# One full-width product for queries times key states, and a different order of the softmax weights' transfers and of GpSimd's splits

## The reference

```python
z = cumlogsumexp(s, axis=tokens);  g = exp(z_shifted - z);  p = exp(s - z)
# per head and token t, with the state hk (64 x 64):
hk = hk * g_t + k_t[:, None] * p_t[None, :];   ok_t = q_t @ hk          # scores against slots
pv = softmax(ok)                                                         # over the 64 slots
hv = hv * g_t[:, None] + p_t[:, None] * v_t[None, :];   ov_t = pv_t @ hv
o = ov * rsqrt(mean(ov**2) + eps) * g_norm * silu(x @ Wg);   out = o @ Wo
```

## Time and profile before

| | |
|---|---|
| time, median of 3 runs | 1357.21 us (1354.89 to 1357.36) |
| the profiled execution | 1352.27 us, its span 1350.5 us |
| PE busy | 1323.4 us (98%) |
| DVE busy | 1055.9 us (78%) |
| ACT busy | 425.9 us (32%) |
| POOL busy | 138.2 us (10%) |
| TensorE clock granted | 0.999 of full speed |

### The profile page before, as it was taken

How to read it: one execution, slowest core, us unless ns; L and a number is a source line. 1 busy time by engine, 2 the same in 40 slices (tenths; PEclk the granted TensorE clock), 3 DMA queues, 4 the chain that set the end, 5 groups by cost and what they waited for, 6 DMA issues and landing times.

```text
span 1350.5 us, 24275 instructions
## 1 busy us (share of the span) xinstructions
PE 1323.4 (98%) x9287; PEld 1096.4 (81%) x9287; DVE 1055.9 (78%) x1675; ACT 425.9 (32%) x1283; POOL 138.2 (10%) x106
## 2 busy tenths in 40 slices
PE   6999999999999999999999999999999999999998
PEld 5788888888888888888888888878888778888886
DVE  8888888888888888888988898888778764535354
ACT  4333323332332233233323333333223423222221
POOL 3012101110120011001101110111100000000000
PEclk9999999999999999999999999999999999999999
DMA  6147555655665565556655655575332620000000
GB/s 187 40 107 176 115 119 131 161 117 110 147 135 126 119 164 127 128 123 156 138 122 122 161 121 116 119 169 117 75 93 44 192 80 0 32 1 31 0 32 32
DMA packets 500559, 144.58 MB, mean 107 GB/s; under 512 B 359648, under 2 KB 491616, under 8 KB 500448
## 3 DMA queue, kind: packets, MB, share of 16 engines
q1 hardware_dynamic: 500448, 143.08, 45.4%
HBM read 85.80 MB, written 57.21 MB: 106 GB/s over the span
## 4 chain that ended last, share of the span: by engine, by line
PE 76%; DVE 10%; SPq 5%; DMA 5%; issue 3%; ACT 0%; POOL 0%; DVEq 0%
PE bank L486 15%; PE bank L488 14%; PE bank L487 14%; PE bank L118 13%; PE bank L1654 6%; PE bank L726 3%; SPq L369 3%; PE bank L709 2%; PE bank L566 2%; PE bank L546 2%; SPq L334 2%; DMA fp_weights<-q 1%; DMA e_tokens<-k_tok_then_wT 1%; PE bank L645 1%; PE bank L714 1%
## 5 line engine op out<-in xcount | busy, mean ns | idle before, releaser
L486 PE MATMUL bank<-wvg_hi,xT_hi 128*128 128x512 f32 x512 | 206.7, 404 | 0.7
L488 PE MATMUL bank<-wvg_hi,xT_lo 128*128 128x512 f32 x512 | 199.9, 390 | 0.0
L487 PE MATMUL bank<-wvg_lo,xT_hi 128*128 128x512 f32 x512 | 199.7, 390 | 0.0
L786 ACT ACTIVATE a_and_v<-bank 128x256 f32<-128x256 f32 x128 | 49.0, 383 | 332.9 <-PE bank L488 332.8
L486 PEld LDWEIGHTS bank<-wvg_hi,xT_hi 128*128 128x128 f32 x512 | 96.2, 188 | 25.5 <-issue 4.2
L488 PEld LDWEIGHTS bank<-wvg_hi,xT_lo 128*128 128x128 f32 x512 | 96.1, 188 | 20.6
L487 PEld LDWEIGHTS bank<-wvg_lo,xT_hi 128*128 128x128 f32 x512 | 96.3, 188 | 17.8
L1103 DVE RECIPROCAL cT<-cT 128x512 f32<-128x512 f32 x32 | 107.0, 3343 | 0.0
L1048 POOL TENSOR_TENSOR rstd<-ssq,neg_half 128x8 f32<-128x8 f32 x32 | 52.4, 1636 | 494.3 <-DVE ssq L1151 494.3
L486 PE MATMUL bank<-wo_hi,oT_hi 128*128 128x512 f32 x256 | 99.8, 390 | 0.0
L488 PE MATMUL bank<-wo_hi,oT_lo 128*128 128x512 f32 x256 | 99.6, 389 | 0.0
(11 more groups left out here) (164 smaller groups left out, 3029.1 us busy)
## 6 DMA issues: line engine op xcount, KB each, us to landing
o_transposed<-o SPq DMA_DIRECT2D x27, 512.0 KB, 3.4
oT_lo<-o_transposed SPq DMA_DIRECT2D x108, 128.0 KB, 3.0
fp_weights<-q SPq DMA_DIRECT2D x28, 318.0 KB, 3.4
e_tokens<-k_tok_then_wT SPq DMA_DIRECT2D x31, 256.0 KB, 2.3
e_tok<-e_tokens SPq DMA_DIRECT2D x124, 64.0 KB, 2.3
c_tokens<-cT SPq DMA_DIRECT2D x31, 256.0 KB, 2.4
cT<-c_tokens SPq DMA_DIRECT2D x124, 64.0 KB, 2.3
w_slots<-p SPq DMA_DIRECT2D x27, 256.0 KB, 2.4
```

The costliest lines, as they stand in the source:

```text
L486: pe.matmul(dst, w_hi, m_hi, start=(k == 0), stop=False)
L487: pe.matmul(dst, w_hi, m_lo, start=False, stop=False)
L488: last = pe.matmul(dst, w_lo, m_hi, start=False, stop=(k == n - 1))
L786: return act.activation(dst, src, ACT.Copy)
```

## The change

Three things are changed. (1) `hk` becomes 128 wide and is set to zero once: the state of head 0 goes to rows 0 to 63, columns 0 to 63, that of head 1 to rows 64 to 127, columns 64 to 127. One copy of ACT becomes two of 64 partitions. L673's 12 products of 64 x 64 by 64 columns per unit become 3 of 128 x 128 by 128 columns. ok of both heads now lies in T0 and is scaled by one DVE instruction instead of two; the parts of hv lie in T1, and their waits move. (2) In SP's queue `load_w` stands right behind `store_w`, and the k weights of the next pair and the loads of e behind it. (3) In units with i = 3 GpSimd's two low parts wait for `s_wm`, the end of L1296.

```diff
-    hk = sb("hk", [P, CH - 1, P])[:, :, 0:M]
+    hk = sb("hk", [P, CH - 1, P])
-    ok_of = [[t[:, c * M:(c + 1) * M] for c in range(CH)] for t in (T0, T1)]
+    ok_of = [T0[:, c * P:(c + 1) * P] for c in range(CH)]
+    hv_of = [T1[:, c * P:(c + 1) * P] for c in range(CH - 1)]
...
             load_q8(u)
-            if i == 2:
-                load_skq(pair, 1)
             store_e(u + 1)
             if u in W_FAR:
                 store_w(u)
+                load_w(u)
+            if i == 2:
+                load_skq(pair, 1)
             load_e(u + 1)
-            if u in W_FAR:
-                load_w(u)
...
             if c:
-                pe.wait_ge(s_hk, 3 * u + c)
+                pe.wait_ge(s_hk, 2 * (3 * u + c))
...
-                if beside is not None and out_bank(u, c) is state_banks(beside)[1]:
-                    pe.wait_ge(s_hv, (CH - 1) * (beside + 1))
...
-            pe.wait_ge(s_hk, 3 * (u + 1))
+            pe.wait_ge(s_hk, 2 * 3 * (u + 1))
             for c in range(1, CH):
-                for a in range(2):
-                    hs = slice(DK * a, DK * (a + 1))
-                    for h in range(2):
-                        ts, ds = slice(64 * h, 64 * (h + 1)), slice(c * P + 64 * h, c * P + 64 * (h + 1))
-                        mm = pe.matmul(ok_of[a][c][ts, :], qT[hs, ds], hk[hs, c - 1, :],
-                                       start=False, stop=True, skip_group_check=True)
+                mm = pe.matmul(ok_of[c], qT[:, c * P:(c + 1) * P], hk[:, c - 1, :],
+                               start=False, stop=True, skip_group_check=True)
...
-                out_product(v, range(CH), u)
+                out_product(v, range(CH))
+            pe.wait_ge(s_hv, 3 * (u + 1))
...
-            copy(hk[:, c, :], state_banks(u)[0][:, 0:M]).then_inc(s_hk, 1)
+            if not u and c == 0:
+                act.wait_ge(s_zero, 1)
+            for a in range(2):
+                rows = slice(64 * a, 64 * (a + 1))
+                copy(hk[rows, c, M * a:M * (a + 1)], hk_bank(u)[rows, 0:M]).then_inc(s_hk, 1)
...
                 pool.wait_ge(s_job, job_count(VG3, u, i))
+                pool.wait_ge(s_wm, u + 1)
                 for k in range(2, KT):
                     lo_vg(pair_of_next(u), k)
...
-            for a in range(2):
-                head = [t.rearrange("p (c a m) -> p c a m", a=2, m=M)[:, :, a, :] for t in (p[:, :], c_tok)]
-                dve.scalar_tensor_tensor(out=head[0], in0=(T0, T1)[a][:, 0:CH * M].rearrange("p (c m) -> p c m", m=M),
-                                         scalar=SCALE, in1=head[1], op0=ALU.mult, op1=ALU.mult).then_inc(s_oks, 1)
+            dve.scalar_tensor_tensor(out=p[:, :], in0=T0[:, :], scalar=SCALE, in1=c_tok,
+                                     op0=ALU.mult, op1=ALU.mult).then_inc(s_oks, 1)
...
+        dve.memset(hk[:, :, :], 0.0).then_inc(s_zero, 1)
```

More of the change, by code:

```diff
@@ L551, in key_sums @@
             if c:
-                pe.wait_ge(s_hk, 3 * u + c)
+                pe.wait_ge(s_hk, 2 * (3 * u + c))
             for a in range(2):
                 hs, at = slice(64 * a, 64 * (a + 1)), slice(M * a, M * (a + 1))
-                mm = pe.matmul(state_banks(u)[0][hs, 0:M], k_tok[:, c, at], e_tok[:, c, at], start=(c == 0), stop=True,
+                mm = pe.matmul(hk_bank(u)[hs, 0:M], k_tok[:, c, at], e_tok[:, c, at], start=(c == 0), stop=True,
                                skip_group_check=True)
             mm.then_inc(s_hkd, 1)
-        def inner_ok(par, chunks):
-            for c in chunks:
-                for a in range(2):
-                    at = slice(M * a, M * (a + 1))
-                    for h in range(2):
-                        ts = slice(64 * h, 64 * (h + 1))
-                        pe.matmul(ok_of[a][c][ts, :], av[par][:, a, c, 0, ts], e_tok[:, c, at],
-                                  start=(c == 0), stop=(c == 0), skip_group_check=True)
         def out_transposes(u, banks):
@@ L582, in w_transposes, with out_product @@
             mm.then_inc(s_trw, 1)
-        def out_product(u, chunks, beside=None):
+        def out_product(u, chunks):
             for c in chunks:
-                if beside is not None and out_bank(u, c) is state_banks(beside)[1]:
-                    pe.wait_ge(s_hv, (CH - 1) * (beside + 1))
                 cols = slice(c * P, (c + 1) * P)
@@ L639, in unit @@
             pe.wait_ge(s_v, (u + 1) * CH)
-            inner_ok(par, range(CH))
+            for c in range(CH):
+                for a in range(2):
+                    at = slice(M * a, M * (a + 1))
+                    for h in range(2):
+                        ts = slice(64 * h, 64 * (h + 1))
+                        pe.matmul(ok_of[c][ts, at], av[par][:, a, c, 0, ts], e_tok[:, c, at],
+                                  start=(c == 0 and a == 0), stop=(c == 0), skip_group_check=True)
             key_sums(u, 1)
@@ L644, in unit @@
                     hs, at = slice(64 * a, 64 * (a + 1)), slice(M * a, M * (a + 1))
-                    mm = pe.matmul(state_banks(u)[1][hs, c * DV:(c + 1) * DV], e_tok[:, c, at], av[par][:, a, c, 1, :],
+                    mm = pe.matmul(hv_of[c][hs, :], e_tok[:, c, at], av[par][:, a, c, 1, :],
                                    start=(c == 0), stop=(c == 0), skip_group_check=True)
@@ L662, in unit @@
                 pe.wait_ge(s_cinv, 1)
-                pe.wait_ge(s_hk, CH - 1)
                 for c in range(CH):
-                    mm = pe.transpose(A[0][:, c * P:(c + 1) * P], c_sum[:, c * P:(c + 1) * P], ident[:, :])
+                    mm = pe.transpose(A[1][:, c * P:(c + 1) * P], c_sum[:, c * P:(c + 1) * P], ident[:, :])
                 mm.then_inc(s_trc, 1)
-            pe.wait_ge(s_hk, 3 * (u + 1))
+            pe.wait_ge(s_hk, 2 * 3 * (u + 1))
             for c in range(1, CH):
-                for a in range(2):
-                    hs = slice(DK * a, DK * (a + 1))
-                    for h in range(2):
-                        ts, ds = slice(64 * h, 64 * (h + 1)), slice(c * P + 64 * h, c * P + 64 * (h + 1))
-                        mm = pe.matmul(ok_of[a][c][ts, :], qT[hs, ds], hk[hs, c - 1, :],
-                                       start=False, stop=True, skip_group_check=True)
+                mm = pe.matmul(ok_of[c], qT[:, c * P:(c + 1) * P], hk[:, c - 1, :],
+                               start=False, stop=True, skip_group_check=True)
             mm.then_inc(s_ok, 1)
@@ L919, in unit @@
                 act.wait_ge(s_trc, 1)
-                copy(c_tok, A[0][:, :]).then_inc(s_ctok, 1)
+                copy(c_tok, A[1][:, :]).then_inc(s_ctok, 1)
             act.wait_ge(s_sub, u + 1)
@@ L1278, in unit @@
                 dve.wait_ge(s_kst, 16 * u)
[L1279 to L1283 removed]
+            dve.scalar_tensor_tensor(out=p[:, :], in0=T0[:, :], scalar=SCALE, in1=c_tok,
+                                     op0=ALU.mult, op1=ALU.mult).then_inc(s_oks, 1)
+            dve.wait_ge(s_oks, u + 1)
             dve.tensor_reduce(mx[:, :], p3, AX.X, ALU.max).then_inc(s_max, 1)
```

15 lines of the change are left out of this document (6 added, 9 removed).

## The result

The changed kernel takes 1367.37 us (median of 4 runs, 1365.14 to 1368.85), the kernel before 1357.28 (4 runs, 1354.89 to 1358.90). The ratio is 1.0072 with a 95% interval of 1.0054 to 1.0091. 1365 was predicted. The profiled execution took 1366.9 us with a span of 1365.2.

A forecast was written before the change was run, and what follows sets the result against it. PE, busy for 98% of the span, was taken as the bound. Product -1.1, second copy +1.8, k weights with w +9.3 and GpSimd's splits -1.8 gave +8.2: profiled 1360.5 us, median 1365, range 1354 to 1375.

The forecast's parts named there:

- The k weights: Units with i = 2: k weights loaded behind w make PE's L555 wait for k; +9.3 us, w's gain included.
- the heart of the matter: Unit 18: ACT's split of k at 641.1, gate(0) and c_turn 2.1 us late, PE's L555 1.8 later.
- The two kinds of unit: Units with i = 2: 10, 14, 18 and 22 lose 1.8 us each; 2, 6 and 26 lose 0.7 each.
- The meeting with GpSimd: Units with i = 2: GpSimd's late split of q still meets DVE's L1243 and L1244; L1244 takes 1.78 in unit 18.
- w (predicted -4): L709, units with i = 2: w's loads start some 1.7 us earlier and PE's stalls for w go, -4 us.
- The product (predicted -1.1): From KTJ's last matmul to QT's second: full-width product takes 1.13 us instead of 1.16, -1.1 us over 32 units.
- +16: Product: by the skill's tiling factor the block's 0.51 us becomes 1.02, +16 us; as rival, 1382 us, chance 0.02.
- The second copy: ACT's copies per key state: PE's third key sum starts 0.05 to 0.06 us late, +1.8 us, bounds 0 and 4.8.
- GpSimd's splits: Units with i = 3: value-weight splits behind L1296 free L1286; PE's VG0 waits 0.26 less, -1.8 us in 7 units.
- its rival: GpSimd's second split goes before L1299, L1076 ends 0.9 later, +6.3 us; total +16.3, 1373.5 us, chance 0.15.
- the collision: Unit 19: GpSimd's two value-weight splits run beside DVE's L1286, which takes 1.57 us and alone would take some 0.7.
- The sum: Whole kernel: -1.1 + 1.8 + 9.3 - 1.8 = +8.2 us, a median of 1365; chance 0.48.

The follow-up runs named there:

- first experiment: The changed kernel with the load of the k weights put back ahead of the store of e in SP's queue: 1353.66 us, ratio 0.9971.
- fourth experiment: The kernel before with the full-width product, its two copies per key state, zeroed hk and moved hv parts alone: 1358.11 us, ratio 0.9999.
- third experiment: The kernel before with only GpSimd's wait for s_wm ahead of its value-weight splits added: 1356.57 us, ratio 0.9991.
- eighth experiment: The changed kernel with the k weights first again in SP's queue and without GpSimd's wait for s_wm: 1350.55 us, ratio 0.9944.
- fifth: The kernel before with w's loads ahead of the loads of e alone, the k weights still first: 1350.27 us, ratio 0.9944.
- seventh experiment: The kernel before with each key state's copy cut in two of 64 partitions, the products unchanged: 1358.92 us, ratio 1.0003.

## Why the prediction was right

**The k weights (predicted +9.3, with the gain of w inside).** The step that was called the heart of the matter held, link by link, within 0.3 us. Behind L709 the units with i = 2 were to lose 9.3 + 4 = 13.3 us to k; PE's three waits come to 7.7 + 3.8 + 2.2 = 13.7. That two of them stand ahead of L555 was half foreseen (L714), and the job for s was not. The first experiment and the changed kernel differ by 13.7. The two kinds of unit that were told apart did not show: all seven lose between 1.2 and 3.3 us, unit 10 most, where gate(0) waited longest for ACT (4.2 us in the table of waits). The meeting with GpSimd that the two kinds were made of is there as assumed: in the kernel before, its split of q holds up the second rounding step in u = 10, 14, 18 and 22, and in the changed kernel it holds up the first or the second in all seven (1.39 to 1.78 us, where each takes 0.82 alone). The sizes by unit were not right, their sum was.

**w (predicted -4).** The cause is right, the size is not: -7.6. The 3.6 of the earlier trace rows were one execution's, and a low one; the three other profiles with that order have 8.5, 6.7 and 5.3. The distance of 4.9 us between the profiled execution and the median was seen, and carried over as a constant. It was in part this wait. Another part goes with the clock: of the 35 runs of the kernel before, the six with a mean granted clock of 0.999, which the profiled execution had, average 1355.0 us, and the three with 0.996 average 1359.5.

**The product (predicted -1.1).** Right: 1.13 against 1.16 us, 31 times -0.035. The gain that the Trainium skill (TensorEngine Tiling (Array Packing), Theoretical Speedup) gives as "up to" the tiling factor would, if had in full, have made it +16, by the prediction's estimate; the fourth experiment, at a ratio of 0.9999, shows no such cost. 24 matmuls of 64 x 64 take 0.51 us here and 6 of 128 x 128 take 0.58, where the full gain would have a factor of two between them: this trace shows little of it.

**The second copy (predicted +1.8, bounds 0 and 4.8).** Mis-sized: 0.12 us a unit, 3.8 in all. The spacing of 0.12 was read from a copy followed by an instruction from SBUF; two copies out of the bank start 0.24 apart. Why they don't overlap stays open; the bank alone is not the reason, since VG0's copy and tanh, both out of a bank, start 0.26 apart at 0.37 long (651.24 and 651.50).

**GpSimd's splits (predicted -1.8).** This step failed, with the wrong sign, though not by its rival: GpSimd's second split did not go ahead of L1289. The sum did not count that L1289 waits for the *first* split, 0.66 us. What was left of the gain in the kernel before, 1.2 us, is gone in the changed one, where VG0 starts 0.34 late. The new product is the likely cause: its scaling starts 0.87 us behind the product's first matmul (671.88 - 671.01) and started 0.64 behind it with the products by head (third experiment, 661.80 - 661.16). No run has GpSimd's wait with the copies but without the product, so this is argued and not shown. And in the company of the two copies the collision was gone anyway, so that the wait costs 3.1 us (first against eighth experiment) where it was to bring 1.8. The prediction's reading that L1286 began only when GpSimd was through is not in the row either: it is recorded from 661.33, and GpSimd ends at 662.35.

**The sum.** By runs: w -7.6, the k weights +13.7, product and copies with the collision gone +0.3 (eighth against fifth), GpSimd's wait +3.1, together +9.5; measured +10.1. Each of these kernels differs from the next by one part, so that the terms add up is so by construction and proves none of them. The prediction had -4, +13.3, +0.7 and -1.8, together +8.2. Its largest term was right. That the total is off by only 2 us is luck beyond that: a gain of w that was 3.6 us too small and a cost of GpSimd's wait that was 4.9 too low nearly cancel, and the copies' miss of 2.0 is hidden because the collision went with them.

## What to carry to other kernels

A load put off in a queue costs nothing where its data are needed late, but everything that stands behind its first reader on an in-order engine waits with it: before such a move, look at what the reader blocks, and move the reader too. A stall on a DMA landing is to be taken from several executions: one profile had 3.6 us of it and another 8.5, and the distance from the profile to the median was the hint. Where two engines exclude each other, a shift of 0.3 us in when one starts decides who waits, so an edit against such a collision is to be tried again whenever another edit has moved either of them.

## What the runs showed of the hardware

- Two ACT copies of 64 x 64 out of the bank start 0.24 us apart and take 218 ns each, against 223 for one of 128 x 64: halving the partitions saves next to nothing.
- When GpSimd has two splits waiting and a DVE instruction of 0.12 us comes between, DVE gets in after the first, but pays 0.66 us for what is left of it (676.80 to 677.58). The other way round GpSimd waits: its pair takes 3.03 instead of 2.55 us. The Trainium skill (SBUF — State Buffer, SBUF: two separate sides) has the exclusion, and these rows agree.
- After PE had stood still for 2.7 us the granted clock went to 0.50, the 1.2 GHz level, for some 4 us in the fourth experiment. In the seventh it did so after a wait of only 1.8 us (at 904.63), and in the third it did not after one of 2.8. The first row is the seventh experiment, the other two are the third:

```profile
906.30:907.50 1.20, 1.20 (x16) 1.20 (x14) 1.13 (x2) 0.00 (x0) 0.00 (x0) 0.50 0.90 242
...
903.00:906.00 3.00, 0.23 (x2) 0.00 (x0) 3.00 (x1) 0.66 (x2) 0.00 (x0) 1.00 0.84 164
906.00:908.00 2.00, 1.97 (x34) 1.98 (x36) 1.20 (x4) 0.00 (x0) 0.00 (x0) 1.00 1.00 270
```

The length of the wait alone does not decide, then; what does stays open. Each of these two drops made its unit 1.6 us longer. One more place shows the same: near the end of the attention, at 1050 to 1070 us, PE waits in every kernel for the feed-forward weights, 2.1 to 3.1 us. The clock then fell to 0.50 for some 4 us in seven of the eleven profiled executions (all but the kernel before, the changed kernel and the third and eighth experiments), without regard to the parts of the change. So it adds to the scatter of every one of these kernels.
